# A two-layer graph network on Trainium2: the matmuls of two message steps as pairs of 64-row matmuls

## What is computed

```python
h = relu(layernorm(x))
edge_in  = concat(h[src], h[dst], edge_features)          # 128 + 128 + 64
h1       = relu(edge_in @ We1 + be1)                      # 32
edge_msg = relu(h1 @ We2 + be2)                           # 128, "msg1"
h2       = relu(concat(h[dst], edge_msg) @ Wn1 + bn1)     # 64
node_msg = relu(h2 @ Wn2 + bn2)                           # 128, "msg2"
x = x + h + segment_sum(node_msg, dst)                    # layer 1
h = relu(layernorm(x))
msg = ((h @ W[r])[etype, src] + b[etype]) * edge_weight   # 8 relations
x = x + h + relu(segment_sum(msg, dst))                   # layer 2
```

## Time and profile before

| | |
|---|---|
| median of 3 runs | 8141.24 us (8136.67 to 8145.61) |
| span of the profiled execution | 8149.0 us |
| TensorE (PE) busy | 6825.6 us, 84% |
| weight loads (PEld) | 5276.0 us, 65% |
| VectorE (DVE) | 3995.9 us, 49% |
| ScalarE (ACT) | 1919.9 us, 24% |
| GpSimd (POOL) | 6074.5 us, 75% |
| gathers of layer 1, of layer 2 | 3128 each, 2984.1 and 2978.3 us busy |
| mean granted TensorE clock | 0.932 of 2.4 GHz |

### The profile page before, as it was taken

How to read it: one execution, slowest core, us unless ns; L and a number is a source line. 1 busy time by engine, 2 the same in 40 slices (tenths; PEclk the granted TensorE clock), 3 DMA queues, 4 the chain that set the end, 5 groups by cost and what they waited for, 6 DMA issues and landing times.

```text
span 8149.0 us, 187072 instructions
## 1 busy us (share of the span) xinstructions
PE 6825.6 (84%) x52884; PEld 5276.0 (65%) x52884; DVE 3995.9 (49%) x13480; ACT 1919.9 (24%) x4919; POOL 6074.5 (75%) x6335
## 2 busy tenths in 40 slices
PE   5999999999999999999967777777778877777777
PEld 4666666666666666666646666666666666666665
DVE  7333333333333333333365555555555556555554
ACT  2333333333333333333330000000000000000001
POOL 5777777777777777777757777777777777777776
PEclk7999999999999999999979888888888888988898
DMA  6333333333333333333322222222222222222222
GB/s 141 82 83 82 81 83 82 83 82 83 82 83 82 82 83 82 83 83 82 82 61 53 53 53 53 53 53 52 53 53 53 53 52 53 52 53 53 53 53 72
DMA packets 797549, 566.94 MB, mean 70 GB/s; under 512 B 481443, under 2 KB 671019, under 8 KB 797292
## 3 DMA queue, kind: packets, MB, share of 16 engines
q0 software_dynamic: 200192, 256.65, 14.6%
q1 hardware_dynamic: 597340, 310.10, 14.5%
HBM read 544.45 MB, written 21.68 MB: 69 GB/s over the span
## 4 chain that ended last, share of the span: by engine, by line
PE 32%; issue 24%; POOL 21%; DMA 20%; DVE 1%; POOLq 1%; SPq 0%; ACT 0%; DVEq 0%; ACTq 0%
PE bank L1130 19%; POOL shared L549 17%; DMA shared<-p_tab,idx 11%; DMA rows_place<-h_tab,idx 6%; PE bank L1143 5%; POOL rows_place L549 4%; PE bank L1132 3%; DMA idx<-in_src_t 2%; PE bank L1054 2%; PE bank L1145 1%; PE bank L1061 1%; PE bank L1080 0%; DMA x_in<-in_x 0%; PE bank L1071 0%; DVE stats L744 0%
## 5 line engine op out<-in xcount | busy, mean ns | idle before, releaser
L549 POOL DMA_INDIRECT shared<-p_tab,idx x3128 | 2984.1, 954 | 959.8 <-issue 826.7
L549 POOL DMA_INDIRECT rows_place<-h_tab,idx x3128 | 2978.3, 952 | 964.3 <-issue 804.4
L1130 PE MATMUL bank<-shared,rows_place 128*128 128x256 f32 x6256 | 1842.2, 446 | 860.4 <-issue 748.1
L1130 PEld LDWEIGHTS bank<-shared,rows_place 128*128 128x128 f32 x6256 | 1296.4, 218 | 1126.6 <-issue 782.8
L959 DVE TENSOR_SCALAR shared<-iota_key,key,w_f 128x256 f32<-128x256 f32 x3128 | 1139.1, 425 | 745.3 <-PE bank L1132 633.1
L704 ACT ACTIVATE x_in<-bank 128x256 f32<-128x256 f32 x782 | 300.8, 385 | 3591.9 <-PE bank L1132 3264.7
L1061 PE MATMUL bank<-h_sb,w_tile 128*128 128x128 f32 x6256 | 907.7, 288 | 22.3 <-DVE h_sb L870 0.8
L1061 PEld LDWEIGHTS bank<-h_sb,w_tile 128*128 128x128 f32 x6256 | 758.5, 191 | 232.4 <-DVE h_sb L870 232.1
L1080 PE MATMUL bank<-wn_half,h_sb 128*128 128x128 f32 x6256 | 890.3, 285 | 0.0
L870 DVE TENSOR_SCALAR h_sb<-bank 128x128 f32<-128x128 f32 x782 | 228.2, 292 | 1315.8 <-PE bank L1054 1294.3
L1143 PE MATMUL bank<-x_in,w_rel_sb 128*128 128x64 f32 x6256 | 862.8, 296 | 0.0
(11 more groups left out here) (105 smaller groups left out, 5379.0 us busy)
## 6 DMA issues: line engine op xcount, KB each, us to landing
rows_place<-in_dst_c SPq DMA_DIRECT2D x782, 192.0 KB
shared<-in_edge_cols SPq DMA_DIRECT2D x782, 128.0 KB
shared<-p_tab,idx POOLq DMA_INDIRECT x3128
rows_place<-h_tab,idx POOLq DMA_INDIRECT x3128
idx<-in_src_t SPq DMA_DIRECT2D x1564, 2.0 KB
qr_w<-qr_tab SPq DMA_DIRECT2D x782, 18.0 KB
x_in<-in_x SPq DMA_DIRECT2D x14, 448.0 KB, 4.7
h_tab<-x_in SPq DMA_DIRECT2D x14, 448.0 KB, 3.0
```

Of the source, the lines that this page charges most:

```text
L549: pool.indirect_dma_start(out=rows_of[s][:, t, :], out_offset=None, in_=table, in_offset=bass.IndirectOffsetOnAxis(ap=idx[s][:, t:t + 1], ...
L1130: pe.matmul(bank[s][:, 0:RW], rows[s][:, t, :], hot_rel[s % 2][:, t, :], start=(t == 0), stop=(t == TC - 1))
```

## The change

The weights lose their blocks of zeros: `w2_pair` holds We2 for four tiles in two columns of blocks (`j % 2`), `wn2_both` holds Wn2 twice, once in each half of the partitions. Each matmul of `sum_msg1` and `sum_msg2` reads only 64 partitions, those of its half `a`, and the two halves of a pair, issued one after the other, write to banks of their own: `ps_msg1` is now columns 0 to 255 of banks 1 and 2, `ps_msg2` of banks 4 and 5. The number of matmuls, their columns and their results stay. To let one instruction read two banks, PSUM is one tensor of eight banks; the banks are numbered a little differently in layer 1. The ReLU of msg1 and the bias of msg2 read and write with a pattern of two halves. One memset of GpSimd goes, another is half as wide, and SP waits for 3 in place of 4.

```diff
-        w2_tile = sb("w2_tile", [P, TC, P])
+        w2_pair = sb("w2_pair", [P, 2, P])
-        wn2_half = sb("wn2_half", [P, 2, P])
+        wn2_both = sb("wn2_both", [P, P])
...
-        bank = [ctx.enter_context(nc.psum_tensor(f"bank{k}", [P, 512], f32)) for k in range(8)]
-        ps_h1, ps_msg1, ps_h2, ps_msg2, ps_tiles, ps_agg = bank[0:6]
+        psum = ctx.enter_context(nc.psum_tensor("psum", [P, 8, 512], f32))
+        bank = [psum[:, k, :] for k in range(8)]
+        ps_h1, ps_h2, ps_tiles, ps_agg = (bank[k] for k in (0, 3, 6, 7))
+        ps_msg1, ps_msg2 = psum[:, 1:3, 0:2 * P], psum[:, 4:6, 0:2 * P]
...
-        ] + [(w2_tile[j * H1:(j + 1) * H1, j, :], we2) for j in range(TC)] \
-          + [(wn2_half[a * H2:(a + 1) * H2, a, :], wn2) for a in range(2)]
+        ] + [(w2_pair[j * H1:(j + 1) * H1, j % 2, :], we2) for j in range(TC)] \
+          + [(wn2_both[a * H2:(a + 1) * H2, :], wn2) for a in range(2)]
...
-            sp.wait_ge(zeroed, 4)
+            sp.wait_ge(zeroed, 3)
...
-            pool.memset(w2_tile[:, :, :], 0.0).then_inc(zeroed, 1)
-            pool.memset(wn2_half[:, :, :], 0.0).then_inc(zeroed, 1)
+            pool.memset(w2_pair[:, :, :], 0.0).then_inc(zeroed, 1)
...
-                act.activation(msg1_sb[:, :], ps_msg1[:, :], ACT.Relu, bias=be2_col[:, 0:1]).then_inc(msg1_done, 1)
+                act.activation(msg1_sb.rearrange("p (a n) -> p a n", a=2), ps_msg1, ACT.Relu, bias=be2_col[:, 0:1]).then_inc(msg1_done, 1)
...
-                dve.tensor_tensor(msg2_sb[:, :], ps_msg2[:, :], bn2_rep[:, :], ALU.add).then_inc(msg2_biased, 1)
+                dve.tensor_tensor(msg2_sb.rearrange("p (a n) -> p a n", a=2), ps_msg2, bn2_rep.rearrange("p (a n) -> p a n", a=2), ALU.add)\
+                   .then_inc(msg2_biased, 1)
...
-                for t in range(TC):
-                    ins = pe.matmul(ps_msg1[:, t * P:(t + 1) * P], w2_tile[:, t, :], h1_sb[:, :], start=True, stop=True)
+                for b in range(2):
+                    for a in range(2):
+                        half = slice(a * 2 * H1, (a + 1) * 2 * H1)
+                        ins = pe.matmul(ps_msg1[:, a, b * P:(b + 1) * P], w2_pair[half, b, :], h1_sb[half, :], start=True, stop=True)
...
-                for t in range(TC):
-                    a, b = t // 2, t % 2
-                    ins = pe.matmul(ps_msg2[:, t * P:(t + 1) * P], h2_sb[:, b * P:(b + 1) * P], wn2_half[:, a, :],
-                                    start=True, stop=True)
+                for b in range(2):
+                    for a in range(2):
+                        half = slice(a * H2, (a + 1) * H2)
+                        ins = pe.matmul(ps_msg2[:, a, b * P:(b + 1) * P], h2_sb[half, b * P:(b + 1) * P], wn2_both[half, :],
+                                        start=True, stop=True)
```

## The result

The changed kernel takes 9258.69 us (median of 4 runs, 9143.07 to 9328.13) against 8142.67 us before (median of 4): 1.137 times as long. By the two shorter runs alone (9143 and 9213 us), which count as the fast ones, it is 1.127 times, with a 95% interval of 1.123 to 1.131. The four runs follow their mean granted TensorE clock: 9143 us at 0.715, 9213 at 0.709, 9305 at 0.696, 9328 at 0.693. Before it was 0.932. The profiled execution is the one of 9328 us, with a span of 9326.0 us, 1177 us over that of before.

What follows compares the result with a forecast made beforehand. The prediction took GpSimd's gathers to bound the kernel, with TensorE hidden behind them. Its terms, 0 + 0 - 1.05 us off the median of 8141.24, gave 8140.2 us, forecast as 8140, range 8122 to 8159.

Steps and rivals of the forecast that it cites:

- What bounds the kernel before: Layer 1 edge loop: GpSimd's gathers set the pace, 1.252 us each, 5.0 us a chunk; TensorE follows with 0.40 us slack.
- The eight matmuls: msg1 and msg2 in layer 1's loop: 0.80 us a call, saving 0.70 us of TensorE per chunk, all hidden.
- rival A: Layer 1 loop: array shape changes cost TensorE 0.57 us a chunk; if pairs save nothing, 133 us slower, 8274 us; 3%.
- The evacuations and the start: ScalarE's and VectorE's reads of two half-filled banks, and GpSimd's fewer memsets at the start: 0 us for each.
- The end of layer 1: After the last gather, three message calls lie on the chain: 1.05 us saved, 0 to 2.2 us by the bounds.
- Rival C: Layer 1 loop: idler TensorE loses clock; at 0.89 nothing moves, at 0.70 470 us more, 8611 us; 3%.
- 0 in the loop: Sum's term for layer 1's loop: TensorE's saving is hidden behind the gathers, so 0 us of the time.
- L1056 no longer waits: Sign of being wrong, tied to rival A: the matmul of the gathered rows (L1054 before) no longer waits for their landing.
- the gap before the gathers varies: Sign of being wrong: GpSimd's 0.30 us gap varies, so GpSimd had been waiting and TensorE's time would count.
- R: Theory of the experiments, not the prediction: 64-row matmuls as such go with the low TensorE clock in layer 1's loop.

Runs made afterwards that it cites:

- e6: The changed kernel with only msg2 in 64-row matmuls, msg1 again in four 128-row matmuls with blocks of zeros: 8138.71 us.
- e8: The changed kernel with six filling 64-row matmuls per chunk, results unused, where TensorE waits for the gathered rows: 8134.88 us.
- e7: The changed kernel with all eight message matmuls on the same rows 0 to 63, output not the reference's: 10891.27 us.
- e3: The kernel before with two of four 128-row matmuls left out of msg1 and of msg2 in every chunk but the first: 8156.85 us.
- e4: The changed kernel with three filling 128-row matmuls per chunk, results unused, where TensorE waits for the gathered rows: 8137.10 us.
- e5: The changed kernel with only msg1 in 64-row matmuls, msg2 again in four 128-row matmuls with blocks of zeros: 8137.86 us.
- e10: The changed kernel with two filling 64-row matmuls per chunk, in different halves of the rows, ahead of L1056: 8160.27 us.

## Why the prediction was wrong, point by point

**What bounds the kernel before: right.** GpSimd issues a gather every 1.25 us and nothing that TensorE saves in the loop is seen while the clock is up. Banks alone, either call alone, and the filled versions all lie within 0.11% of before, though TensorE's busy time in 200 to 4000 us went from 3494 us down to 3307 (e6) or up to 3708 (e8).

**The eight matmuls: right in kind, undersized.** A call takes 0.71 us at the full clock; I took 0.80, between 0.43 and 1.16. By their own length the two calls save 0.88 us a chunk, not 0.70. The sentence on the Trainium skill's "TensorEngine Tiling (Array Packing)" ("Theoretical Speedup", up to 2x) would have given 1.15; the trace has 1.6x and lies between the two, nearer to my 0.70, and e7 shows where the gain comes from. TensorE's chunk gets shorter by less than its calls, though, which is rival A.

**The evacuations and the start: right** (L650 687 ns, L881 692 ns, as before). **The end of layer 1:** with the clock up (e8), first L1068 of the last chunk to the copy of agg is 4084.17 - 4075.75 = 8.42 us, against 4095.62 - 4086.66 = 8.96: 0.54 us saved, half of my 1.05. The calls themselves saved more; but at the very end of e8 the clock had fallen already, and its last L1096 and L1104 took 0.57 and 0.63 us, where the same two took 0.43 and 0.41 before. It decides nothing.

**Rival A, drains at changes of shape: there, at about half its price.** The prediction read the one change of shape that it looked at, L1054 to L1088, as free, because the two groups overlap. Starts tell it better than ends, which are modelled. The calls of before, at the full clock:

```profile
2005.06 1.16 PE L1061 MATMUL bank<-h_sb,w_tile 128*128 128x128 f32 x8
2006.05 0.31 PE L1096 MATMUL bank<-fold_tiles,tile_sums 128*128 128x32 f32 x2
2006.20 1.14 PE L1080 MATMUL bank<-wn_half,h_sb 128*128 128x128 f32 x8
2007.26 0.66 PE L1071 MATMUL bank<-shared,wn_msg 128*64 128x256 f32 x4
```

From the start of msg1 to the start of `sum_h2` (L1071, in the changed kernel L1075) it is 2.20 us before and 565.10 - 563.47 = 1.63 us with pairs. That is 0.57 us less a chunk and not the 0.88 by which the calls are shorter, so 0.3 us were lost in between, where I had put 0.57 for this rival. In the single records the last matmul of a group and the first of the next start 112 ns apart before, between L1061, L1096 and L1080, which have one shape; with pairs it is 202 and 206 ns at the same two borders, and the two records of the fold between them start 133 ns apart in place of 31. L1054 to L1088 (L1056 to L1093) has 205 ns in either kernel, so that change wasn't free either. This agrees with the rule of the Trainium skill's "TensorEngine Tiling (Array Packing)" ("Key Properties"), by which changing the tiling mode drains TensorE. At the full clock all of it is hidden, as the prediction said. At the lower clock it isn't: it is most of what sets the 6.84 us of a chunk apart from the 6.39 of e3, where the calls are as long.

**Rival C is the step that failed,** and with it the term "0 in the loop" of the sum, which holds only while the clock is up. C had the mechanism and its point: below a clock of 3.93 / 5.03 = 0.78 TensorE becomes the bound. It had the wrong clock. I read 0.89 off the loop of layer 2 because TensorE idles as much there, and applied it as a mean that stretches the work once. Three things were wrong in that. The clock has two levels, so the row to price it by is the lower level itself: at 0.50 my 3.93 us would have been up to 7.9 us, and it is 6.84, 1.81 above the period. Second, a fall needn't be short: with e3's matmuls the clock is back after 17 us at most, with 64-row pairs it stays down for up to 1400 us, though TensorE is then busy all the time. The rule that idleness brings the clock down and work brings it up is that of the Trainium skill's page "TensorE: Matmul & The Clock Gate" ("Part 1: The HAM clock gate"); the first half agrees with the trace (TensorE was 81% busy at the full clock before the fall at 624 us, and 92% without any fall in the kernel before), the second doesn't hold here: 1419 us of 1419 busy at 0.50, and 3800 of 3800 in e7. Third, short falls are hidden by the four slots of gathers and long ones aren't, so the cost isn't proportional to the mean clock: 0.91 cost 15 us (one run), 0.54 cost 1170 us. Priced by the lower level, with the 6.84 us that were measured, C would have read 782 x 1.81 = 1415 us, 9556 us, as its far end, and the trace of before held no row by which a fall to it could be excluded: no 64-row matmul ran there. Three chances in a hundred were far too few for that.

**What showed it** was in the list of the prediction: L1056 no longer waits, and the gap before the gathers varies. I had put these down for A and for a misreading of GpSimd, not for the clock.

**Shown and not shown.** That the loss is the clock's: shown by e4 and e8, which change nothing but added work. That matmuls of 64 rows, and not only the time that TensorE works, decide whether the clock comes back: shown by e7 beside before, where the calls are equally long, and by e3. That it takes both calls: shown by e5 and e6. What in 64-row matmuls keeps the clock down isn't shown. One rival to R was not tested: that it isn't the 64 rows as such but how much of the array is at work on the whole. At the lower clock the two calls of e7 use half as many rows as those of before in the same time, and the pairs spread the rows of e3 over a longer chunk, so both comparisons fit it as well, and so do e8 to e10, in which 64-row work brings the clock back. Not shown either is what ended the low stretches now and then (at 495 us in the changed kernel it rose in the middle of L1056, after chunks like any other).

## What to carry to other kernels

An engine off the critical path that is made to do less can lose its clock, and then become the path. Where TensorE's load falls, price the lower level of the clock for the whole loop, compare it with the period of the engine that bounds it, and look how long a fall would last; if the work changes shape as well, rows of the old shape don't tell that, and each new border between shapes costs TensorE time too. Where the bound is elsewhere, leave TensorE's spare work (zeros included) alone, or fill the pause and check the granted clock by stretch.

## What the runs showed of the hardware

- Two 64-row fp32 matmuls in different halves of the rows run side by side: a call of four takes 0.71 us in place of 1.16 at 2.4 GHz, 1.23 in place of 2.08 at 1.2 GHz. On the same rows each costs as much as one of 128 rows (e7, 2.08 us a call at 1.2 GHz).
- A change between matmuls of 128 and of 64 rows takes time: the first of the new shape starts 202 to 206 ns after the last of the old one at 2.4 GHz, where neighbours of one shape start 112 ns apart. The fold between the two calls thus cost 0.3 of the 0.88 us that the pairs saved.
- Which of two orders the four were issued in made no difference (0.71 and 0.72 us).
- TensorE busy without a pause stayed at 1.2 GHz for 1419 us with 64-row pairs, and for a whole loop of over 6600 us with 64-row matmuls on the same rows.
- Three extra 128-row matmuls a chunk, or six of 64 rows, brought the clock from 0.54 (200 to 4000 us) to 1.00 and the time from 9259 to 8137 and 8135 us; a single one of 128 rows brought it to 0.98.
- Reads of two half-filled PSUM banks by one ScalarE or VectorE instruction take as long as reads of one full bank (687 and 692 ns).
